# Splitting the Q and K projections into three bfloat16 parts: from ScalarE and VectorE to GpSimd, in a gated cross-attention block with mixture-of-experts routing

## What is computed

```python
qh = (q @ Wq.T); kh = (k @ Wk.T); vh = (v @ Wv.T)        # 16 heads each
attn = softmax(qh * scale @ kh^T, axis=2)                # over the 512 queries
attn = attn / sum(attn, axis=-1)                         # then over the 1601 keys
x = x + tanh(g_xattn) * ((attn @ vh) @ Wo.T)
probs = softmax(layernorm(x) @ router_w.T); top 2 of 8
x = x + tanh(g_ffn) * sum of gate * (gelu(row @ w1[e]) @ w2[e])
```

## Time and profile before

| | |
|---|---|
| median of 3 runs | 1903.37 us (1903.24 to 1906.2) |
| profiled execution, own time | 1903.8 us |
| its span, first to last instruction | 1902.0 us |
| mean granted TensorE clock | 0.975 |
| TensorE / VectorE / ScalarE / GpSimd busy | 1672.8 / 1407.2 / 1289.1 / 557.8 us |
| attention of eight batches, first to last exponential | about 56 to 1314 us |
| one iteration of batches 1 to 6 | 157.0 us |
| experts | from about 1370 us to the end |

### The profile page before, as it was taken

How to read it: one execution, slowest core, us unless ns; L and a number is a source line. 1 busy time by engine, 2 the same in 40 slices (tenths; PEclk the granted TensorE clock), 3 DMA queues, 4 the chain that set the end, 5 groups by cost and what they waited for, 6 DMA issues and landing times. The chain is left out here.

```text
span 1902.0 us, 31292 instructions
## 1 busy us (share of the span) xinstructions
PE 1672.8 (88%) x9774; PEld 889.5 (47%) x9888; DVE 1407.2 (74%) x2269; ACT 1289.1 (68%) x3634; POOL 557.8 (29%) x837
## 2 busy tenths in 40 slices
PE   5589899889988989989988898886299999999997
PEld 3223233233323323323322332212299999999997
DVE  1488999999989999899998999996344444444443
ACT  2499989989999998999999999995011111111111
POOL 5141152235135135223413512213212222222222
PEclk9799999999999999999999999998599999999999
DMA  5915414432522441532343152114512222222221
GB/s 152 228 35 142 120 56 117 119 89 85 155 80 71 136 130 51 133 121 77 97 143 80 56 150 73 45 67 157 198 31 36 36 36 36 38 34 38 36 36 28
DMA packets 124933, 168.64 MB, mean 89 GB/s; under 512 B 14320, under 2 KB 102256, under 8 KB 124816
## 3 DMA queue, kind: packets, MB, share of 16 engines
q1 hardware_dynamic: 102064, 136.77, 26.1%
q0 software_dynamic: 13344, 17.90, 5.5%
q10 hardware_dynamic: 9408, 12.58, 1.8%
HBM read 117.96 MB, written 49.24 MB: 88 GB/s over the span
## 5 line engine op out<-in xcount | busy, mean ns | idle before, releaser
L659 ACT ACTIVATE w_all<-scores,negmax 128x512 f32<-128x512 f32 (+1 forms) x1664 | 1120.3, 717 | 48.6 <-DVE negmax L810 42.4
L810 DVE TENSOR_REDUCE negmax<-scores 128x2 f32<-128x1024 f32 (+1 forms) x832 | 1000.6, 1215 | 105.0 <-PE scores L549 100.4
L549 PE MATMUL scores<-q_stack,w_all 128*128 128x512 bf16 (+1 forms) x1550 | 477.8, 385 | 131.6 <-ACT w_all L659 114.2
L562 PE MATMUL acc<-w_all,vz 128*32 128x512 f32 (+1 forms) x3328 | 445.0, 607 | 8.8 <-POOL vz L934 7.7
L549 PEld LDWEIGHTS scores<-q_stack,w_all 128*128 128x128 bf16 (+1 forms) x1664 | 112.8, 100 | 605.4 <-ACT w_all L659 460.1
L659 ACT ACTIVATION_READ_ACCUMULATOR w_all<-scores,negmax 128x1 f32 (+1 forms) x1664 | 393.0, 236 | 0.0
L1128 ACT ACTIVATE hidden<-ps_hidden 128x512 f32<-128x512 f32 x142 | 84.8, 597 | 430.0 <-PE ps_hidden L1091 430.0
L934 POOL TENSOR_TENSOR vz<-w_all,rz 128x68 f32<-128x68 f32 (+1 forms) x416 | 124.6, 299 | 835.3 <-DVE rz L796 816.6
L1091 PEld LDWEIGHTS ps_hidden<-rows_t,w_sb 128*128 128x128 f32 x2272 | 267.4, 194 | 5.7 <-DVE rows_t L1155 1.7
L1091 PE MATMUL ps_hidden<-rows_t,w_sb 128*128 128x128 f32 x2272 | 268.2, 277 | 1.1 <-DVE rows_t L1155 1.0
L1104 PE MATMUL ps_y<-w_sb,hidden 128*128 128x256 f32 x1136 | 256.8, 379 | 0.0
(11 more groups left out here) (134 smaller groups left out, 1008.2 us busy)
## 6 DMA issues: line engine op xcount, KB each, us to landing
w_all<-k_parts SPq DMA_DIRECT2D x256, 200.1 KB, 3.5
q_stack<-q_parts SPq DMA_DIRECT2D x256, 64.0 KB, 3.3
w_all<-in_ctx_t SPq DMA_DIRECT2D x8, 1601.0 KB, 7.9
k_parts<-parts SPq DMA_DIRECT2D x42, 300.0 KB, 2.8
w_all<-in_w ACTq DMA_DIRECT2D x12, 1024.0 KB, 12.0
rows<-routed SPq DMA_DIRECT2D x71, 129.0 KB, 2.0
q_parts<-parts SPq DMA_DIRECT2D x14, 384.0 KB, 3.1
k_parts<-parts SPq DMA_DIRECT2D x14, 300.8 KB, 3.0
```

Of the source, the lines that this page charges most:

```text
L549: mm = pe.matmul(scores[0:r, 2 * (u % SLOTS) + j % 2, :], k_stack[:, g, j, lt * P:lt * P + r], q_stack[:, g, j, :], start=True, stop=True)
L562: mm = pe.matmul(acc[32 * j:32 * j + 32, :], vz[0:r, s % RING, j, :], probs[0:r, s % RING, j, :], start=(lt == 0), stop=(lt == LT - 1))
L659: e = act.activation(probs[0:r, s % RING, j, :], scores[0:r, 2 * (u % SLOTS) + j % 2, :], ACT.Exp, bias=negmax[0:r, u % 4, j % 2:j % 2 + 1 ...
L810: dve.tensor_reduce(negmax[0:r, u % 4, :], scores[0:r, 2 * (u % SLOTS):2 * (u % SLOTS) + 2, :], AX.X, ALU.max, negate=True).then_inc(negma ...
```

## The change

From batch 0 on (in every iteration but the first, preparing one), a q or k chunk goes another way:

- ScalarE writes the projection, scaled for q, as float32 into `resid` and counts `fill_taken`. It waits for `parts_ready` of two chunks before (the buffer `resid` is free), and no longer for `parts_stored`.
- VectorE does nothing for it.
- GpSimd writes the high part (a sum with zero, bfloat16 out), subtracts it from `resid` in place (float32 out), both in the chunk's own step; in the next step it writes the middle part and then the low part. It waits for its own instructions between dependent ones, and for `parts_stored` before the high part.

```diff
@@ ScalarE, take @@
-                if name in ("q", "k"):
+                if name in ("q", "k") and not it.first:
                     c, at, n = it.chunk(name, i)
                     act.wait_ge(fill_ready, it.made(name, i))
-                    if not it.first:
-                        wait(act, parts_stored[c % 2], ((b + 1) * (CHUNKS // 2) + at // 2) * 16)
+                    act.wait_ge(parts_ready, (b + 1) * CHUNKS + at - 1)
+                    act.activation(resid[:, at % 2, 0:n], spare[:, 0:n], ACT.Copy,
+                                   scale=D ** -0.5 if name == "q" else 1.0).then_inc(fill_taken, 1)
+                elif name in ("q", "k"):
+                    c, at, n = it.chunk(name, i)
+                    act.wait_ge(fill_ready, it.made(name, i))
                     act.activation(parts_of(it, c)[:, 0, 0:n], bank(it, name, i)[:, 0:n], ACT.Copy,
                                    scale=D ** -0.5 if name == "q" else 1.0).then_inc(high_ready, 1)
@@ VectorE, run @@
-                        if f and f[0] not in ("v", "x_turn") and p == (f[0] in ("q", "k")):
+                        if f and f[0] not in ("v", "x_turn") and (it.first or f[0] not in ("q", "k")) and p == (f[0] in ("q", "k")):
                             take(it, *f)
@@ GpSimd @@
+            def split(it, at, n, part, k):
+                done = 3 * (it.b * CHUNKS + at)
+                if k == 1:
+                    pool.wait_ge(split_step, done + 2)
+                pool.tensor_tensor(part[:, k, 0:n], resid[:, at % 2, 0:n], zero[:, 0:1].to_broadcast([P, n]),
+                                   ALU.add).then_inc(split_step, 1)
+                pool.wait_ge(split_step, done + (1, 3)[k])
+                if k == 0:
+                    pool.tensor_tensor(resid[:, at % 2, 0:n], resid[:, at % 2, 0:n], part[:, 0, 0:n],
+                                       ALU.subtract).then_inc(split_step, 1)
@@ GpSimd, run: one step after the chunk's @@
-                        pool.wait_ge(middle_ready, (b + 1) * CHUNKS + at + 1)
+                        if it.first:
+                            pool.wait_ge(middle_ready, at + 1)
+                        else:
+                            split(it, at, n, parts_of(it, c), 1)
                         pool.tensor_tensor(parts_of(it, c)[:, 2, 0:n], resid[:, at % 2, 0:n], parts_of(it, c)[:, 1, 0:n],
                                            ALU.subtract).then_inc(parts_ready, 1)
@@ GpSimd, run: the chunk's own step @@
                         pool.wait_ge(fill_taken, it.made(name, i))
-                        pool.tensor_tensor(parts_of(it, c)[:, 1, 0:n], resid[:, at % 2, 0:n], zero[:, 0:1].to_broadcast([P, n]),
-                                           ALU.add).then_inc(middle_ready, 1)
+                        if it.first:
+                            pool.tensor_tensor(parts_of(it, c)[:, 1, 0:n], resid[:, at % 2, 0:n], zero[:, 0:1].to_broadcast([P, n]),
+                                               ALU.add).then_inc(middle_ready, 1)
+                        else:
+                            wait(pool, parts_stored[c % 2], ((b + 1) * (CHUNKS // 2) + at // 2) * 16)
+                            split(it, at, n, parts_of(it, c), 0)
```

More of the change, by code:

```diff
@@ L306, in attention_and_routing @@
         middle_ready = sem("middle_ready")
+        split_step = sem("split_step")
         parts_ready = sem("parts_ready")
```

## The result

| | before | after |
|---|---|---|
| median | 1903.66 us (4 runs) | 1927.55 us (1926.92 to 1934.08, 4 runs) |
| profiled execution, own time | 1903.8 | 1934.08 |
| ratio | | 1.013, 95% interval 1.0107 to 1.0154 |

The change costs 24 us; forecast was no change, and the range ended at 1917. The profiled execution is the slowest of the four, 30.3 us above the one before. Its mean granted TensorE clock is 0.963, against 0.967 and 0.968 in the other three; why is part of the finding.

The account below looks back on a forecast made before the run. Experts bound by TensorE, attention by ScalarE and VectorE together. From 1903.8 us, 6 x (-3.4 - 0.3 + 4.3) = +3.6 and batch 0 -4.4, less 0.4 for the median, gave 1902.6 us; range 1888 to 1917.

Parts of the forecast that it names:

- steps 12 to 18: Batches 1 to 6, beside layer norm: GpSimd's added work makes `vz` late, 25.4 us against 21.09, 4.3 us more per iteration.
- the low level: Batch 0, step 10: TensorE after standing still may run at 0.50 of 2.4 GHz, a lag up to 5.0 us, not 3.4.
- VectorE's relief: Steps 0 to 11: five k subtractions leave VectorE's queue, 3.4 us off per iteration, bounds 2.3 and 4.6.
- The 0.96 us wait for the output projection: Step 8: VectorE's wait goes since `spare` comes free earlier; with 2.3 us for the subtractions, together 3.3 us.
- The check by batch 7: Second working of steps 0 to 11: batch 7 without chunks, 34.25 us, plus five takes gives 36.15, 3.2 us below 39.35.
- GpSimd's queue: Steps 12 to 16: v(12) to v(17) grows from 16.03 to 20.6 us with the added copies and subtractions.
- Steps 19 to 30: Two q subtractions go at steps 24 and 26: 0.3 us off per iteration, between zero and ScalarE's idle 0.76 us.
- Batch 0: Stall moves from ScalarE's to GpSimd's queue, store time unchanged: 4.5 us off by step 10, 4.4 off in sum.
- Rival 1: GpSimd's queue is the new bound, worse than costed: steps 12 to 16 stretch costs 5.2 us, 1917.8 us, chance 0.25.
- Rival 2: VectorE's relief carries: 4.6 + 0.8 us off, stretch only 3.7 on, 1887 us, chance 0.2.
- Rival 3: Steps 24 to 28: VectorE's routing products wait behind GpSimd, about 2 us per iteration, 1914.6 us, chance 0.1.

Follow-up runs that it names:

- load_only: Kernel before plus two more GpSimd instructions per chunk (float32 subtraction and bfloat16 copy into scratch), ScalarE and VectorE as they were: 1944.84 us, ratio 1.0201.
- keep_busy: Kernel after with unit 1's scores in steps 14 to 18 of batches 0 to 6 computed three times over: 1917.67 us, ratio 1.0058.
- relief_only: Kernel after without its two new GpSimd instructions per chunk, so the high part is never written: 1885.11 us, ratio 0.9888.
- the spread kernels: Kernel after with chunks out of steps 10 to 19, no long fills in neighbouring steps: 0.9922; also storing first in batch 0: 0.9858 (ratios to kernel before).
- the second profile: The kernel after run once more, unedited: 1929.89 us, ratio 1.0144, profiled execution 1925.46 us.

## Why the prediction was wrong

- **The step that failed is a missing term.** The sum priced steps 12 to 18 at 4.3 us, the length by which TensorE's wait for `vz` grows, and put nothing for what that wait does to TensorE afterwards. It lowered TensorE's granted clock, 3.2 us a time around step 19, and this hit most of batches 1 to 6: 16.0 of the 30.3 us in the profiled execution. The text had the low level as a price for batch 0 only, though the earlier trace rows showed it behind a standstill, and no rival had it for the other batches. `load_only` brings these low clocks about with ScalarE and VectorE untouched, and `keep_busy`, which fills TensorE's waits, takes them all away. Without them the kernel would have stayed inside the range: the measured terms without the clock give about 1915, and so does the ratio of `keep_busy`, 1.0058.
- **Low clocks at step 0 were missing too**, 1.4 us a time, 5.4 us in the profiled execution. They do not come from late `vz`: `relief_only` and the spread kernels, with no crowding on GpSimd, have them as well. Their cause is open.
- **VectorE's relief was over-sized.** 3.4 us taken, 2.47 measured in `relief_only` and batch 5. The lower bound, five times 0.46 = 2.3, was nearly the answer. The 0.96 us wait for the output projection was counted as wholly going. In the kernel before, TensorE had waited only 0.33 us for VectorE's subtraction of step 7; the rest is its own time for the projection, 1.99 us before and 1.89 after, behind the scores of the step. In the kernel after, by VectorE's queue in order of time, half of the wait is still there:

```profile
577.29 0.75 DVE L732 SCALAR_TENSOR_TENSOR x<-spare,tgx,x 128x512 f32<-128x512 f32 x1 [0.50 <-PE spare L513]
```

  The check by batch 7 did agree, but batch 7 also lacks VectorE's statistics of the next `x_in`, instructions of 0.42 us that batch 3 has in steps 6, 10 and 11; that difference was overlooked, so the agreement of the two workings was chance.
- **GpSimd's queue was right**: 20.52 us for 20.6, hand-over and subtraction to 0.01 us. That steps 12 to 18 came out at 25.37 for 25.4 is closer than its terms: in batch 5 they are 1.59, 20.52 and 3.26 us for 1.4, 20.6 and 3.4, and the misses cancel.
- **Steps 19 to 30** were 37.53 against 37.31, 0.22 up instead of 0.3 down. `relief_only` has 37.25, so the q relief is worth 0.06, and GpSimd's two further instructions a chunk cost 0.28 there. The forecast read this stretch off a window 1.2 us too long; ScalarE's idle time, 0.76 us, is the same in the right one.
- **Batch 0** gained 2.9 us by step 10 for 4.5, since the store landed 1.6 us later, and the whole batch 0.9 for 4.4. Behind its crowded step 16 the clock was low too (step 18 at 5.20 us, 2.98 before); in the second profile it was not, and batch 0 gained 3.0.
- Rival 1 named the right engine and sign but the wrong mechanism: nothing in the queue cost over what was summed. Rival 2 did not occur. Rival 3, routing behind GpSimd, did not either: of VectorE's products of 128x32 in steps 19 to 30, those that met the last 150 ns of a GpSimd product took 193 to 204 ns, against 158 to 177 for the same ones before, and none took longer. With the right terms the queue, less VectorE's relief, gives 6 x 2.0 = 12 us; with 0.9 off for batch 0 that is the 1915 above.

## What to carry over

Before work goes to an idle engine, look at what else stands in its queue and who waits for that: an average of 29% busy hid five steps at 100%. Here the same split cost 1.3% beside layer norm, and gained 0.7% (13.3 us) with the chunks a few steps later. Where a kernel keeps TensorE nearly busy, price every new wait of TensorE twice, once for its length and once for a lower clock after it; iterations that should be alike, compared with each other, give that second price. And when one wait is removed, take from the queue only the time that the removed instruction held up the next one, until the next cause in line has been read.

## What was not expected of the hardware

- A standstill of TensorE of 6.4 us in five pieces over some 25 us lowered its clock for about 7 us, in five of six batches in one execution and four of six in the next; the batches' busy times in steps 12 to 18 up to there are the same to 0.1 us. In all nine the clock fell 22.9 to 23.5 us after the start of step 12. What decides which batch is hit is open. The Trainium skill (TensorE: Matmul & The Clock Gate, Part 1: The HAM clock gate) says that what the gate observes by is free-running and does not start with the work, which would let equal batches be hit unequally; no run here was made to test it.
- At step 0, TensorE's pauses about the end of a batch are in the kernel before too, where the clock never fell in batches 1 to 7 of its one profiled execution. In the other kernels that ran here it fell there in up to five batches of one execution. Why is open; only that repeating matmuls in the pauses ends it was shown.
- Matmuls repeated for nothing won back more than half of what the change cost (`keep_busy`: ratio 1.006 instead of 1.013 and 1.014), without lengthening the stretch they were put in.
